# Attention kernel: score masks moved from TensorE to GpSimd, weighed sums one pair of score blocks later, eight exponential buffers

## The reference

```
q, k, v = (h @ W.T + b) as (batch, head, 1024, 32)
scores = einsum('bhqd,bhkd->bhqk', q, k) / sqrt(32)
scores = where(causal, scores, -inf)
att = softmax(scores, axis=-1)
out = einsum('bhqk,bhkd->bhqd', att, v)
```

## Time and profile before

| | |
|---|---|
| median of 3 runs | 3254.94 us (3254.62 to 3255.73) |
| profiled execution | 3244.23 us, span from first to last instruction 3242.5 us |
| mean granted TensorE clock | 0.959 |
| TensorE busy | 3027.9 us, 93% of the span |
| GpSimd, VectorE, ScalarE busy | 1337.8, 1474.0, 1071.8 us |
| time of the profile's steady group | 40.21 us |

### The profile page before, as it was taken

How to read it: one execution, slowest core, us unless ns; L and a number is a source line. 1 busy time by engine, 2 the same in 40 slices (tenths; PEclk the granted TensorE clock), 3 DMA queues, 4 the chain that set the end, 5 groups by cost and what they waited for, 6 DMA issues and landing times. The chain is left out here.

```text
span 3242.5 us, 47773 instructions
## 1 busy us (share of the span) xinstructions
PE 3027.9 (93%) x17972; PEld 2139.0 (66%) x17972; DVE 1474.0 (45%) x2773; ACT 1071.8 (33%) x1442; POOL 1337.8 (41%) x507
## 2 busy tenths in 40 slices
PE   3999899989999996999999999999999968999997
PEld 2888788878878885555555555555555546767775
DVE  4211312231222111666666666666666446666664
ACT  1222222121222110455555555555555512111110
POOL 2212422142232121466666666666666613333332
PEclk7999999999999998899999999999999979999997
DMA  6443433342343545544444444444444062444431
GB/s 222 182 155 142 165 126 131 116 155 110 129 149 113 198 162 149 114 107 106 108 107 105 110 106 106 105 106 106 106 106 105 15 209 78 152 121 117 127 120 52
DMA packets 149746, 405.00 MB, mean 125 GB/s; under 512 B 17357, under 2 KB 52613, under 8 KB 148569
## 3 DMA queue, kind: packets, MB, share of 16 engines
q1 hardware_dynamic: 149512, 402.95, 42.4%
q10 hardware_dynamic: 80, 0.03, 0.0%
HBM read 271.20 MB, written 131.20 MB: 124 GB/s over the span
## 5 line engine op out<-in xcount | busy, mean ns | idle before, releaser
L852 ACT ACTIVATE prob<-ps_s 128x1024 f32<-128x1024 f32 (+3 forms) x768 | 615.4, 810 | 482.2 <-PE ps_s L956 308.2
L875 DVE TENSOR_REDUCE part_high<-ps_r 128x1 f32<-128x512 f32 (+3 forms) x1024 | 542.4, 584 | 380.4 <-PE ps_r L923 363.1
L823 POOL TENSOR_TENSOR added<-added,prob 128x2048 f32<-128x2048 f32 (+1 forms) x192 | 666.8, 3473 | 55.0 <-ACT prob L852 31.9
L609 PE MATMUL ps_u<-h_hi,w_hi 128*128 128x512 f32 x1536 | 604.0, 393 | 0.0
L609 PE MATMUL ps_u<-h_hi,w_lo 128*128 128x512 f32 x1536 | 599.3, 390 | 0.0
L609 PE MATMUL ps_u<-h_lo,w_hi 128*128 128x512 f32 x1536 | 599.0, 390 | 0.0
L424 POOL TENSOR_TENSOR w_lo<-w_raw,w_hi 128x1024 fp32r<-128x1024 f32 x96 | 231.0, 2407 | 843.1 <-ACT w_hi L471 843.1
L923 PE MATMUL ps_r<-k_st,q_st 96*128 96x512 f32 (+2 forms) x1536 | 541.9, 415 | 30.5 <-DMA v_sb<-v_tok 27.4
L953 PE MATMUL ps_s<-q_st,k_st 97*128 97x512 f32 (+2 forms) x1536 | 526.8, 410 | 16.1 <-DMA q_st<-shift 7.7
L546 DVE SCALAR_TENSOR_TENSOR qk_lo<-ps_u,bias_col,qk_hi 128x512 fp32r<-128x512 f32 x128 | 96.1, 751 | 671.9 <-ACT qk_hi L447 671.9
L953 PEld LDWEIGHTS ps_s<-q_st,k_st 97*128 97x128 f32 x1536 | 287.2, 197 | 135.2 <-issue 94.8
(11 more groups left out here) (152 smaller groups left out, 3054.8 us busy)
## 6 DMA issues: line engine op xcount, KB each, us to landing
q_st<-qk_split SPq DMA_DIRECT2D x96, 512.0 KB, 7.6
k_st<-qk_split SPq DMA_DIRECT2D x96, 512.0 KB, 13.9
w_raw<-w_cols SPq DMA_DIRECT2D x72, 512.0 KB, 3.5
qk_split<-qk_hi SPq DMA_DIRECT2D x64, 512.0 KB, 2.7
qk_split<-qk_lo SPq DMA_DIRECT2D x64, 512.0 KB, 3.4
xn<-in_L_attn_x SPq DMA_DIRECT2D x8, 2048.0 KB, 12.5
v_tok<-v_out SPq DMA_DIRECT2D x32, 512.0 KB, 2.7
wm<-in_L_wmod SPq DMA_DIRECT2D x8, 2048.0 KB, 8.4
```

Of the source, the lines that this page charges most:

```text
L609: last = nc.tensor.matmul(ps_u[u % 2][:], w[:, m, k], h[:, k, tok], start=k == 0 and j == 0, stop=k == KT - 1 and j == 2)
L823: nc.gpsimd.tensor_tensor(total[:, :, off:], so_far, prob[:, k % PBUF, :, off:], ALU.add).then_inc(added_up, 1)
L852: nc.scalar.activation(prob[:, k % PBUF, 2 * pair:2 * pair + 2, off:], ps_s[pair][:, :, off:], ACT.Exp, scale=SCALE).then_inc(exp_done, 1)
L875: nc.vector.reduce_max(dst, bank_of(use)[:, 0:width], AX.X).then_inc(row_free, 1)
```

## The change

- The mask matmuls of pass 2 go. The exponentials of the diagonal blocks are taken of unmasked scores, and GpSimd zeroes the wrong half of their 128 x 128 diagonal part for all four heads by one `affine_select` (`mask`), eight a group. The adds of GpSimd for blocks 4 to 7 and the weighed sums of pairs 2 to 5 wait for `masked` instead of for the exponentials. Row tiles of pass 1 keep their masks.
- `weigh` is called two pairs behind the scores instead of one (HOPS = 2): after pair 0 comes `weigh` of pair 4 of the group before, after pair 1 that of pair 5 and `sum_low`, after pair 2 `weigh` of pair 0 and `sum_high`.
- `prob` has eight buffers, numbered through all groups.
- ScalarE's copies of outputs and sums, and the banks of the two sums, move with the later calls. SyncE stores the upper output half at the start of the next group, ahead of the wait for `weighed`.

```diff
@@ -658,10 +658,13 @@
     NSTEP = len(steps)
     PAIRS = NSTEP // 2
     LONG = (QC * CT)
-    PBUF = 6
+    PBUF = 8
     RB = 3
     ADDS = LONG - 1
-    assert QC == 2 and NSTEP % PBUF == 0 and steps[LONG][1] == 0
+    HOPS = 2
+    MASKS = QC * CT
+    FIRST = LONG - CT
+    assert QC == 2 and steps[LONG][1] == 0 and steps[FIRST][1] == CT
 
     high = [(i, ch, h) for i in range(CT, TT) for ch in range(QC) for h in range(HG)]
     low = [(i, 0, h) for i in range(CT) for h in range(HG)]
@@ -691,8 +694,8 @@
         slots = per_slot(t) if t < NG else [[]] * (2 * NSTEP)
         for n, items in enumerate(slots):
             ring += items
-            if n in (3, 7) and t > 0:
-                ring.append(("sum", t - 1, 0 if n == 3 else 1))
+            if n in (7, 11) and t > 0:
+                ring.append(("sum", t - 1, 0 if n == 7 else 1))
     place = {use: n for n, use in enumerate(ring)}
     rows_upto, sums_upto = {}, {}
     for use in ring:
@@ -732,7 +735,7 @@
         shift_ready = [sem(f"shift_ready{i}") for i in range(QC)]
         shift_loaded = [sem(f"shift_loaded{i}") for i in range(QC)]
         score_done, exp_done = sem("score_done"), sem("exp_done")
-        weighed, o_done, o_copied = sem("weighed"), sem("o_done"), sem("o_copied")
+        masked, weighed, o_done, o_copied = sem("masked"), sem("weighed"), sem("o_done"), sem("o_copied")
         added_up, sum_done, sum_copied = sem("added_up"), sem("sum_done"), sem("sum_copied")
         att_stored = [sem(f"att_stored{i}") for i in range(QC)]
         sums_stored = [sem(f"sums_stored{i}") for i in range(QC)]
@@ -740,6 +743,12 @@
 
         def bank_of(use):
             return ps_r[place[use] % RB]
+
+        def buffer_of(t, k):
+            return (NSTEP * t + k) % PBUF
+
+        def masked_upto(t, k):
+            return MASKS * t + k - FIRST + 1
 
         def offset(k):
             ch, j = steps[k]
@@ -773,6 +782,8 @@
             load(1)
             load_shift(0, 1)
             for t in range(NG):
+                if t > 0:
+                    store_att(t - 1, 1)
                 if t + 2 < NG:
                     if t > 0:
                         sp.wait_ge(weighed, PAIRS * t)
@@ -783,9 +794,9 @@
                 load_shift(t, 0)
                 if t > 0:
                     store_sums(t - 1, 1)
-                store_att(t, 1)
                 if t + 1 < NG:
                     load_shift(t + 1, 1)
+            store_att(NG - 1, 1)
             store_att(NG - 1, 0)
             store_sums(NG - 1, 0)
             store_sums(NG - 1, 1)
@@ -808,19 +819,47 @@
                 nc.gpsimd.memset(k_st[i][SHIFT_ROW:SHIFT_ROW + 1].bitcast(F32), 1.0).then_inc(const_ready, 1)
             pool.wait_ge(const_ready, SLOTS + 1)
 
+            def mask(t, k):
+
+                ch, j = steps[k]
+                pool.wait_ge(exp_done, 2 * (NSTEP * t + k + 1))
+                off = j * P - ch * BANK
+                own = prob[:, buffer_of(t, k), :, off:off + P]
+                nc.gpsimd.affine_select(out=own, in_=own, compare_op=ALU.is_ge, fill=0.0, base=0,
+                                        pattern=[[0, HG], [1, P]], channel_multiplier=-1).then_inc(masked, 1)
+
+            def add(t, k):
+
+                total, off = added[t % 2], offset(k)
+                if k < FIRST:
+                    pool.wait_ge(exp_done, 2 * (NSTEP * t + k + 1))
+                else:
+                    pool.wait_ge(masked, masked_upto(t, k))
+                if k == 1:
+                    if t > 1:
+                        pool.wait_ge(sum_done, sums_upto["sum", t - 2, 1])
+                    so_far = prob[:, buffer_of(t, 0)]
+                else:
+                    pool.wait_ge(added_up, ADDS * t + k - 1)
+                    so_far = total[:, :, off:]
+                nc.gpsimd.tensor_tensor(total[:, :, off:], so_far, prob[:, buffer_of(t, k), :, off:], ALU.add).then_inc(added_up, 1)
+
             for t in range(NG):
-                total = added[t % 2]
-                for k in range(1, LONG):
-                    off = offset(k)
-                    pool.wait_ge(exp_done, 2 * (NSTEP * t + k + 1))
-                    if k == 1:
-                        if t > 1:
-                            pool.wait_ge(sum_done, sums_upto["sum", t - 2, 1])
-                        so_far = prob[:, 0]
-                    else:
-                        pool.wait_ge(added_up, ADDS * t + k - 1)
-                        so_far = total[:, :, off:]
-                    nc.gpsimd.tensor_tensor(total[:, :, off:], so_far, prob[:, k % PBUF, :, off:], ALU.add).then_inc(added_up, 1)
+                add(t, 1)
+                add(t, 2)
+                mask(t, 4)
+                add(t, 3)
+                mask(t, 5)
+                mask(t, 6)
+                add(t, 4)
+                mask(t, 7)
+                add(t, 5)
+                add(t, 6)
+                mask(t, 8)
+                add(t, 7)
+                mask(t, 9)
+                mask(t, 10)
+                mask(t, 11)
 
         @block.scalar
         def _(act):
@@ -849,18 +888,19 @@
                         act.wait_ge(sum_done, sums_upto["sum", before // NSTEP, 0])
                 for pair in range(2):
                     act.wait_ge(score_done, 2 * (NSTEP * t + k) + pair + 1)
-                    nc.scalar.activation(prob[:, k % PBUF, 2 * pair:2 * pair + 2, off:], ps_s[pair][:, :, off:], ACT.Exp, scale=SCALE).then_inc(exp_done, 1)
+                    nc.scalar.activation(prob[:, buffer_of(t, k), 2 * pair:2 * pair + 2, off:], ps_s[pair][:, :, off:], ACT.Exp, scale=SCALE).then_inc(exp_done, 1)
 
             for t in range(NG):
                 for k in range(NSTEP):
                     exponents(t, k)
-                    if k == 1 and t > 0:
+                    if k == 0 and t > 0:
+                        copy_o(t - 1, 1)
+                    if k == 3 and t > 0:
                         copy_o(t - 1, 0)
                         copy_sums(t - 1, 0)
-                    if k == 3 and t > 0:
+                    if k == 5 and t > 0:
                         copy_sums(t - 1, 1)
-                    if k == LONG + 1:
-                        copy_o(t, 1)
+            copy_o(NG - 1, 1)
             copy_o(NG - 1, 0)
             copy_sums(NG - 1, 0)
             copy_sums(NG - 1, 1)
@@ -946,14 +986,11 @@
 
                 ch, j = steps[k]
                 off = min(offset(k), BANK - 2 * P)
-                on_diagonal = j >= ch * CT
                 if 2 * (NSTEP * t + k) > 0:
                     pe.wait_ge(exp_done, 2 * (NSTEP * t + k - 1) + pair + 1)
                 for h in range(2):
                     last = nc.tensor.matmul(ps_s[pair][:, h, off:], k_st[t % SLOTS][:, 2 * pair + h, j * P:(j + 1) * P],
-                                            q_st[t % SLOTS][:, 2 * pair + h, ch * BANK + off:(ch + 1) * BANK], start=True, stop=not on_diagonal)
-                    if on_diagonal:
-                        last = nc.tensor.matmul(ps_s[pair][:, h, offset(k):offset(k) + P], mask_b[:], ident_b[:], start=False, stop=True)
+                                            q_st[t % SLOTS][:, 2 * pair + h, ch * BANK + off:(ch + 1) * BANK], start=True, stop=True)
                 last.then_inc(score_done, 1)
 
             def weigh(t, p):
@@ -962,13 +999,16 @@
                     pe.wait_ge(o_copied, 2 * t)
                 if 2 * p == LONG:
                     pe.wait_ge(o_copied, 2 * t + 1)
-                pe.wait_ge(exp_done, 2 * (NSTEP * t + 2 * p + 2))
+                if 2 * p < FIRST:
+                    pe.wait_ge(exp_done, 2 * (NSTEP * t + 2 * p + 2))
+                else:
+                    pe.wait_ge(masked, masked_upto(t, 2 * p + 1))
                 for k in (2 * p, 2 * p + 1):
                     ch, j = steps[k]
                     off, end = offset(k), j == (ch + 1) * CT - 1
                     for h in range(HG):
                         part = slice(h * HD, (h + 1) * HD)
-                        last = nc.tensor.matmul(ps_o[part, off:], v_sb[t % SLOTS][:, j, part], prob[:, k % PBUF, h, off:], start=j == 0, stop=end)
+                        last = nc.tensor.matmul(ps_o[part, off:], v_sb[t % SLOTS][:, j, part], prob[:, buffer_of(t, k), h, off:], start=j == 0, stop=end)
                 last.then_inc(weighed, 1)
                 if end:
                     pe.wait_ge(weighed, PAIRS * t + p + 1)
@@ -981,7 +1021,7 @@
                 for k in range(LONG, NSTEP):
                     off = offset(k)
                     for h in range(HG):
-                        last = nc.tensor.matmul(bank_of(use)[h * HD:(h + 1) * HD, off:], ones[:], prob[:, k % PBUF, h, off:], start=k == LONG, stop=k == NSTEP - 1)
+                        last = nc.tensor.matmul(bank_of(use)[h * HD:(h + 1) * HD, off:], ones[:], prob[:, buffer_of(t, k), h, off:], start=k == LONG, stop=k == NSTEP - 1)
                 last.then_inc(sum_done, 1)
 
             def sum_high(t):
@@ -1004,14 +1044,16 @@
```

(14 more changed lines are left out.)

## The result

The changed kernel takes 3571.76 us (3563.83 to 3579.04, 3 runs) against 3254.94 before, a ratio of 1.097 (95% interval 1.094 to 1.101). The forecast was slower, 3353 us in a range of 3292 to 3440. The direction and the stall were right; the time lies 132 us above the range.

What follows compares the result with a forecast made beforehand. TensorE's own order was taken to bound each 40.21 us group. 29 groups x (2.2 longer + 1.3 clock) = 101.5, three groups at -1.7 = -5, last selects +1: +98 in all, giving 3353 us, range 3292 to 3440.

Steps and rivals of the forecast that it cites:

- the stall: Before pair 4, TensorE waits 3.8 us (bounds 3 to 4.6) for the lower half's shift row, in 29 groups.
- The masks: Score pairs 2 to 5: removing the mask matmuls gives back 2.7 us a group, limited by VectorE's row tiles.
- 0.65 us a select: GpSimd: each of eight new selects a group takes 0.65 us (bounds 0.56 to 1.17), with no TensorE wait due.
- ScalarE gains no wait: ScalarE: eight buffers are just what sums two pairs late need, so no added wait.
- T+11.5: SyncE: the load is issued 11.5 us after the group's start T, 5.7 us later than before.
- T+27.2: TensorE reaches pair 4 27.2 us after the group's start T; shift0 lands at T+30.9.
- Rival 1: Transfer queue: small shift transfers are not held up by the load, only the masks' gain is left; 3201 us, chance 0.12.
- The border: Pair 5 to the next group's start can't be shorter than 5.35 us; some 1.1 us of gain go there.
- a fall in three of four groups: Behind the pair 4 stall the granted clock falls, costing 1.3 us a group (bounds 0 and 1.75).
- The prediction's 42.4 us: Length of a group with a load, stall and border wait included, clock fall not; 2.2 us more than 40.21.
- Rival 3: Clock stays low through pair 4, W2 and pair 5, costing up to 5 us a group; 3460 us, chance 0.10.
- The 3366 us: Total if, by the skill's rule, all 29 groups pay 1.75 us for a clock fall.

Runs made afterwards that it cites:

- e5: Changed kernel with the shift0 transfers issued ahead of the load and twelve instead of eight lower-half row tiles done a group ahead: 3168.82 us, ratio 0.975.
- e3: Kernel before with the score masks left out altogether, everything else as before: 3190.50 us, ratio 0.9825.
- e4: Changed kernel with GpSimd's selects left out, diagonal not masked, waits kept: 3562.15 us, ratio 1.096.
- e1: Changed kernel with SyncE issuing the four shift0 transfers ahead of the load of q, k and v: 3326.64 us, ratio 1.025.
- e2: Kernel before with only the load of the group after next delayed until pair 1's score blocks are done: 3610.95 us, ratio 1.113.
- e6: Changed kernel with only twelve instead of eight lower-half row tiles done a group ahead: 3423.85 us, ratio 1.054.
- e10: Changed kernel with the score masks back on TensorE and no selects, later sums kept: 3523.15 us, ratio 1.083.
- e7: Changed kernel with the weighed sums one pair late as before, masks still on GpSimd: 3280.30 us, ratio 1.010.
- e8: Changed kernel with sums one pair late, masks on GpSimd, and twelve instead of eight lower-half row tiles done a group ahead: 3309.87 us, ratio 1.018.
- e12: Changed kernel with shift0 ahead of the load and nine instead of eight lower-half row tiles done a group ahead: 3194.31 us, ratio 0.984.

## Why the prediction was wrong

**The masks.** Predicted 2.7 us a group from spacing between starts and VectorE's tiles; measured 40.21 - 37.59 = 2.62 (e5), of which 0.17 is the border wait that before had, so 2.45. e3 gives 1.93 + 0.70 - 0.17 = 2.46. Near enough, and the recorded 236.8 us of busy time would have misled: it is 7.4 us a group.

**GpSimd.** 0.65 us a select predicted, 0.633 measured, no cost (e4). TensorE waits for one once, 3.9 us, at the stage's end, where the prediction had 1 us. "ScalarE gains no wait" was wrong: between 1400 and 2500 us it waits three times for GpSimd's adds, 14.5 us in all. Without the selects (e4) it has no such wait, and the time is within 0.3%.

**The load and the stall.** Predicted 3.8 us; 4.25 in the group shown and 4.4 at most. Shift0 is held up by the load, which e1 shows by taking it out of that place and e2 by making the stall in a kernel without the change. The issue came at T+16.2, not T+11.5: pair 0 and W4 run at the lower clock and take 8.70 + 2.59 us instead of 4.92 + 1.64. Pair 4 was due as much later, at T+32.2 instead of T+27.2, so this error left the stall's length alone. Rival 1 (small transfers pass the load) falls. The Trainium skill, "DMA: Bandwidth & Descriptors", section "Queues, rings and completion order", says that each transfer engine takes its descriptors in ring order. The trace agrees: the store behind the load took 16.4 us to land, and the wait for shift0 ended 20.2 us behind the load's issue. That a later small transfer may be done first, as the section also allows, no run here shows.

**The border.** Predicted 1.1 us of wait, measured 1.51. Right as a wait: pair 5's start to the next group's was put at 5.35 us and takes 5.35 in e1, of which TensorE works 3.8 us, not 4.2. What the prediction left out is that it, too, brings the clock down: e6 takes out this wait alone and gains 148 us.

**The clock: the step that failed.** "I choose a fall in three of four groups: 1.3 us a group (bounds 0 and 1.75; more is a rival)." It counted one fall, and took its length from a row in the last stage, where dense matmuls followed. In the attention stage there are two falls a group. The clock is 0.50 all through pair 4 after the stall and 0.52 in pair 0 after the border. Against full clock, pair 0 loses 8.70 - 4.92 = 3.8 us, W4 2.59 - 1.64 = 0.95, pair 4 7.58 - 4.3 = 3.3 (4.3 being the prediction's; 4.53 at full clock in e1), W2 3.21 - 1.71 = 1.5: 9.5 us in this group, not 1.3. The prediction's 42.4 us, with these 9.5, 0.5 more of stall, 0.4 more from pair 5 to the border (its first slot still ran slow) and 0.2 more in pairs 2 and 3, make 53.0; the group has 52.95. Rival 3, a clock that stays low through pair 4 and W2, came nearest (3460 us) and had 0.10; it lacked the second fall. The Trainium skill, "TensorE: Matmul & The Clock Gate", section "HAM oscillation — how this bites in real kernels", tells of a kernel whose every tile starts at the lower clock. The trace agrees: all 21 stalls between 1400 and 2500 us brought a fall, 19 of them before pair 4 had begun. The 3366 us that I hung on it used the wrong length.

A row in the trace of before could have said so. The attention stage began at half clock; these windows are the second half of pair 0 of group 0 and what follows, in the kernel before:

```profile
1320.00:1325.00 5.00, 5.00 (x15) 3.05 (x15) 3.16 (x5) 2.69 (x3) 0.00 (x0) 0.50 1.04 211
1325.00:1330.00 5.00, 5.00 (x24) 3.58 (x27) 3.70 (x9) 3.40 (x4) 4.79 (x2) 0.70 1.05 207
```

TensorE was busy all the time there and the clock stayed at 0.50 for another 5 us and more. I took the length of a fall from another stage's work instead.

Why the clock takes 10 us and more to come back in this mix of score matmuls and row tiles, when a 4.26 us idle in the last stage cost 3.5 us, no run here settles. The masks on TensorE don't explain the 20 us of e2: e10 has them too, and its clock is low for 10 to 14 us. What stands behind the idle differs. In e7 it is the dense W4, and the low stretch is 3.5 us each time; in e8 it is the same W4, and the stretch is 3.5 us in ten cases and about 14 in eight. In e2 the short W3 and pair 5 stand before the next long weighed sum, and the clock is back 1.3 us behind that. I didn't vary this by itself, so that dense work right behind the idle shortens the low stretch is a guess.

## What to carry to other kernels

Before moving the work that a prefetch waits for, look at what is queued behind the prefetch: here a 2 KB transfer behind 3.5 MB landed when the 3.5 MB did, and the fix was to issue it first. Price a new idle stretch of TensorE at its length plus what the following work loses at half clock, taken from rows of the same stage; in e1 a fall behind 1.56 us of idle cost another 4.75 us, though the clock didn't fall each time (e1, e8). A change that looks bad as a whole may hold a good part: the same masks and the same later sums gain 2.5% once both waits are gone.

## What the runs showed of the hardware

- Idle stretches of TensorE of 1.5 to 1.6 us brought the granted clock down in all 21 groups of the changed kernel and in 20 of 26 of e1, those of 1.87 us in all 26 of e7; those of 0.98 to 1.17 us in none of 28 (e12).
- The length of the idle alone doesn't decide: 2.3 us left the clock at 1.00 in 8 of 26 cases (e8). What else does isn't shown.
- Behind such a stretch score matmuls and row tiles ran at 1.2 GHz for 7 to 14 us (after, e1, e6, e10), and mostly for 20 to 24 us in e2.
- A GpSimd select of 4 x 128 columns of 128 partitions takes 633 ns, against 292 for 128 columns: 0.89 ns for each further column.
